# A fused attention, recurrence and expert kernel: 32 of 128 recurrence units moved into the attention rounds, expert rows scatter-added to the residual

## The reference, cut to what matters

```python
x = x + xattn0(layernorm(x), ctx, ...)      # q, k from ctx; softmax(q k'); mixes the columns of layernorm(x)
x = x + moe0(layernorm(x), ...)             # 16 experts, each token goes to its best 2
x = x + mamba(ctx, z=layernorm(x), ...)     # convolution, step sizes, recurrence over 512 positions, gate silu(z)
x = x + ffn1(layernorm(x), ...)             # two experts of 8, chosen once for all tokens, width 2048

def step(state, inp):                       # the recurrence, 16 states for each of 512 channels
    d, b, c, u = inp
    dA = jnp.exp(d[..., None] * A)
    state = state * dA + (d * u)[..., None] * b[:, None, :]
    y = jnp.einsum('bdn,bn->bd', state, c)
```

## Time and profile before

| | us |
|---|---|
| median of 3 runs | 1596.02 (1595.16 to 1596.70) |
| span of the profiled execution | 1594.7 |
| sequence stage (to the first routing step on DVE) | 262.2 |
| routing, to the first scan | 32.3 |
| the 8 units ahead | 28.1 |
| tile loop, 120 units | 429.7 |
| combine | 106.8 |
| from there to the end | 735.6 |

### The profile page before, as it was taken

One profiled execution on the slowest core, in us unless ns is written; L12 is line 12 of the kernel. 1 busy time (PEld: TensorE's weight loads), 2 busy tenths in 40 slices (PEclk: granted clock), 3 DMA queues, 4 the chain that ended last, 5 costly groups with the idle time before them and its releaser, 6 DMA issues.

```text
span 1594.7 us, 18873 instructions
## 1 busy us (share of the span) xinstructions
PE 1391.5 (87%) x6080; PEld 1030.4 (65%) x6080; DVE 936.9 (59%) x1186; ACT 709.8 (45%) x1303; POOL 784.0 (49%) x607
## 2 busy tenths in 40 slices
PE   6988983588899989897166999999999999999998
PEld 3535532566666656664166787878787887878786
DVE  2677767999999999998683224241414224241413
ACT  4445433266766776665143333333333333333332
POOL 0000000788888988885631445444544545444442
PEclk9898895699999999999555999999999999999999
DMA  3202214477977987863655900010000100010000
GB/s 105 108 26 81 107 53 165 158 240 257 315 257 234 319 269 264 281 198 125 218 198 203 364 14 0 0 66 1 14 0 13 52 13 0 0 53 0 0 0 26
DMA packets 78202, 191.29 MB, mean 120 GB/s; under 512 B 10856, under 2 KB 15752, under 8 KB 77120
## 3 DMA queue, kind: packets, MB, share of 16 engines
q1 hardware_dynamic: 64832, 157.03, 29.3%
q0 software_dynamic: 6400, 20.98, 4.1%
q10 hardware_dynamic: 6912, 12.59, 2.2%
HBM read 152.55 MB, written 38.01 MB: 119 GB/s over the span
## 4 chain that ended last, share of the span: by engine, by line
PE 58%; DVE 22%; issue 10%; ACT 4%; POOL 3%; DMA 3%; ACTq 0%; SPq 0%; DVEq 0%; POOLq 0%
PE decay L1675 22%; PE bank L1664 21%; DVE decay L1247 11%; DVE S L1256 4%; PE bank L1474 2%; PE decay L1430 2%; PE bank L1437 1%; DVE XH L1114 1%; PE bank L1494 1%; PE bank L1534 1%; PE decay L1484 1%; PE bank L1619 1%; POOL Y L767 1%; PE bank L1561 1%; PE decay L1480 1%
## 5 line engine op out<-in xcount | busy, mean ns | idle before, releaser
L1387 DVE CAST HFH<-HF 128x512 fp32r<-128x512 f32 x128 | 59.0, 461 | 496.7 <-ACT HF L1045 496.7
L815 POOL TENSOR_TENSOR W2L<-W2R,W2H 128x512 fp32r<-128x512 f32 x128 | 172.5, 1347 | 348.2 <-ACT W2H L1040 348.2
L728 POOL TENSOR_TENSOR S<-DTU,Bb 128x1024 f32<-128x1024 f32 x128 | 304.7, 2401 | 25.1 <-DVE row_hot L1229 21.7
L1247 DVE TENSOR_TENSOR_SCAN decay<-decay,S 128x1024 f32<-128x1024 f32 x128 | 292.9, 2288 | 0.5 <-ACT decay L892 0.5
L1664 PE MATMUL bank<-XSH,W1H 128*128 128x512 f32 x512 | 202.9, 396 | 4.2 <-POOL W1L L811 4.2
L1675 PE MATMUL decay<-W2H,HFH 128*128 128x512 f32 x512 | 200.4, 391 | 5.3 <-DVE HFL L1389 5.3
L1664 PE MATMUL bank<-XSH,W1L 128*128 128x512 f32 x512 | 203.0, 396 | 0.0
L1664 PE MATMUL bank<-XSL,W1H 128*128 128x512 f32 x512 | 202.3, 395 | 0.0
L1675 PE MATMUL decay<-W2L,HFH 128*128 128x512 f32 x512 | 199.9, 390 | 0.0
L1675 PE MATMUL decay<-W2H,HFL 128*128 128x512 f32 x512 | 199.7, 390 | 0.0
L811 POOL TENSOR_TENSOR W1L<-W1R,W1H 128x512 fp32r<-128x512 f32 x128 | 171.1, 1337 | 49.6 <-ACT W1H L1031 49.6
(11 more groups left out here) (212 smaller groups left out, 2102.3 us busy)
## 6 DMA issues: line engine op xcount, KB each, us to landing
WGU<-in_L_ffn_gate_w SPq DMA_DIRECT2D x48, 384.0 KB, 3.8
WGU<-in_L_ffn_up_w SPq DMA_DIRECT2D x48, 384.0 KB, 5.1
WD<-in_L_ffn_down_w SPq DMA_DIRECT2D x48, 384.0 KB, 4.9
Bb<-bc_rows SPq DMA_DIRECT2D x32, 512.0 KB, 7.9
Cb<-bc_rows SPq DMA_DIRECT2D x32, 512.0 KB, 9.7
...
```

The lines of the kernel that those rows point to most:

```text
L728: pool.tensor_tensor(S[u % NP][:], DTU[:, ds(b, 1), c, :].to_broadcast([P, PAIR, L]), Bb[j][:], ALU.mult).then_inc(dbu_ready, 1)
L815: pool.tensor_tensor(W2L[f % 2][:], W2R[:, ds(e, 1), f, :].rearrange("p e d -> p (e d)"), W2H[f % 2][:].bitcast(F32), ALU.subtract).then_i ...
L1247: dve.tensor_tensor_scan(flat, flat, S[u % NP][:].rearrange("p i l -> p (i l)"), 0.0, ALU.mult, ALU.add).then_inc(scan_done, 1)
```

## The change

The program is laid out anew as far as the combine stage.

- Batch 0's projections, convolution and step sizes run alone at the start. Then come 4 rounds, written out in place of the loop. Round b holds the attention of batch b, the recurrence inputs of batch b+1 (none in round 3), and 8 units of batch 0 (`ROUND`), 32 in all (`EARLY`).
- In the rounds PE uses three banks in turn for every product (`jobs`, `bank_of`); a job waits until the job three places ahead of it has been taken out. The four `decay` banks and YS are the units'.
- Both layer norms of a round are applied on ACT (4 instructions of 128x512 each) with a shift from POOL in place of DVE's. Of the step sizes' five passes DVE keeps two (`correction`); POOL has the other three (`step_sizes`), in its list ahead of the round's next unit but two.
- Units of batch 0 have four buffers of S, Bb and Cb, the later ones eight.
- Routing lays out the slot's token and its weight: 64 small DVE steps of 128x48 in place of four of 128x768, and a product of 96 columns in place of 48.
- 8 units still run ahead of the first tile, 80 are spread over the 48 tiles (1 or 2 each), 8 (`TAIL`) follow the last tile.
- x1 is stored as rows. A tile's result, scaled by the slot's weight, is added to those rows by an indirect accumulating DMA issued on POOL (`add_rows`), each of which waits for the one before. `store_y`, `gather_y`, `add_first`, `add_second` and the tile's copy of its index column are gone; four loads of 1 MB bring x2.

```diff
-PAD = 6200
+PAD = 14200
+TAIL = 8
+LATE = 5
...
+        EARLY = UB
+        ROUND = EARLY // B
+        AHEAD = EARLY + 2 * HP
         ALL = B * UB
-        cuts = [AHEAD + (ALL - AHEAD) * j // SLOT_TILES for j in range(SLOT_TILES + 1)]
+        cuts = [AHEAD + (ALL - AHEAD - TAIL) * j // SLOT_TILES for j in range(SLOT_TILES + 1)] + [ALL]
...
+        jobs = mamba_in(0) + mamba_out(0)
+        for b in range(B):
+            jobs += four("e", b)[:2] + four("v", b)[:2] + four("e", b)[2:] + four("v", b)[2:]
+            jobs += (mamba_in(b + 1) if b + 1 < B else []) + four("p", b) + four("o", b)
+            jobs += (mamba_out(b + 1) if b + 1 < B else []) + four("n", b) + [("score", b, 0)]
+        job_at = {job: i for i, job in enumerate(jobs)}
...
+            def step_sizes(b):
+
+                dt, dtu, rl = DT[:, b], DTU[:, b], XP[:, :, TAPS - 1:]
+                pool.wait_ge(nd_ready, b + 1)
+                pool.wait_ge(r_ready, b * DC + DC)
+                pool.tensor_tensor(rl, rl, ZZ[:], ALU.subtract).then_inc(size_made, 1)
+                pool.wait_ge(ln_ready, b + 1)
+                pool.wait_ge(size_made, 2 * b + 1)
+                pool.tensor_tensor(dt, rl, dt, ALU.add).then_inc(size_made, 1)
+                pool.wait_ge(size_made, 2 * b + 2)
+                pool.wait_ge(u_spilled, b * DMA + DMA)
+                pool.wait_ge(xd_ready, b + 1)
+                pool.tensor_tensor(dtu, dt, dtu, ALU.mult).then_inc(dt_ready, 1)
...
+            products(0, 3)
+            for b in range(B):
+                n = b * ROUND
+                products(n + 3, n + ROUND)
+                scale_and_shift1(2 * b + 2)
+                products(n + ROUND, n + ROUND + 2)
+                if b + 1 < B:
+                    scale_and_shift1(2 * b + 3)
+                    step_sizes(b + 1)
+                products(n + ROUND + 2, n + ROUND + 3)
...
+            def add_rows(j):
+
+                pool.wait_ge(yt_ready, j + 2)
+                if j:
+                    pool.wait_ge(yt_added, j * DMA)
+                pool.indirect_dma_start(out=x2_rows, out_offset=bass.IndirectOffsetOnAxis(ap=slot_dst[:, j:j + 1], axis=0),
+                                        in_=YT[j % 2][:], in_offset=None, compute_op=ALU.add).then_inc(yt_added, DMA)
...
                 gate_by_up(j)
+                if j >= 2:
+                    add_rows(j - 2)
                 if j + 2 < SLOT_TILES:
                     gather(0, j + 2)
-
-
-            def gather_y(b, k, count):
...
-                pool.tensor_copy(gcol[n % 2][:], slot_tok[:, ds(j, 1)]).then_inc(gcol_ready, 1)
-                wait_apart(pool, gcol_ready, j + 1)
...
-            def gather_y(b, k, count):
-
-                if b >= 2 and k == 0:
-                    pool.wait_ge(y_loaded[b % 2], b // 2 * (TOP * T * DMA))
-                pool.tensor_copy(pcol[b % 2][k][:], pos[:, k, b * T:(b + 1) * T]).then_inc(pcol_ready, 1)
-                pool.wait_ge(pcol_ready, count)
-                for t in range(T):
-                    pool.indirect_dma_start(
-                        out=(Y1, Y2)[k][b % 2][:, t, :], out_offset=None, in_=y_dram,
-                        in_offset=bass.IndirectOffsetOnAxis(ap=pcol[b % 2][k][:, t:t + 1], axis=0)).then_inc(y_loaded[b % 2], DMA)
...
+                decays(n + 5, n + 6)
+                if more:
+                    silu_u(b + 1)
+                decays(n + 6, n + 7)
+                if more:
+                    take_qk(b + 1)
+                    take_xd(b + 1)
+                decays(n + 7, n + 8)
+                norm_x1(b)
+                if more:
+                    size_abs(b + 1)
+                for t in range(T):
+                    take_turned("n", b, t, XNT)
+                if more:
+                    size_exp(b + 1)
+                take_scores(b)
+                if more:
+                    size_ln(b + 1)
+                    norm_x(b + 1)
+                decays(n + 8, n + 9)
...
-                act.activation(YT[:], DOWN[:], ACT.Copy, scale=0.5).then_inc(yt_ready, 1)
-
-            def store_y(j0, n):
-                j = j0 + n
-                act.wait_ge(yt_ready, j + 2)
-                act.dma_start(y_dram[ds(j * P, P), :], YT[:]).then_inc(yt_stored, DMA)
...
+                if j >= 2:
+                    act.wait_ge(yt_added, j * DMA - DMA)
+                act.activation(YT[n % 2][:], DOWN[:], ACT.Copy, scale=slot_w[:, j:j + 1]).then_inc(yt_ready, 1)
...
+                if more:
+                    convolve(b + 1, (2, 3))
+                unit(n + 5)
+                add_x(b, 0)
+                add_x(b, 1)
+                unit(n + 6)
+                add_x(b, 2)
+                add_x(b, 3)
+                statistics_x1(b)
+                unit(n + 7)
+                if more:
+                    positive_part(b + 1)
+                    statistics_x(b + 1)
+                    correction(b + 1)
...
+                for t in range(NT):
+                    dve.tensor_scalar(tile_hot[:, k, t, 0, :], iota_j[:], jf[:, k, t:t + 1], tokid[:, t:t + 1],
+                                      ALU.is_equal, ALU.mult)
+                    ins = dve.tensor_scalar(tile_hot[:, k, t, 1, :], iota_j[:], jf[:, k, t:t + 1], rwt[:, k, t:t + 1],
+                                            ALU.is_equal, ALU.mult)
+            ins.then_inc(hot_ready, 1)
...
-            def add_first(b):
-
-                dve.wait_ge(x1_loaded, max(b + 1, 2) * DMA)
-                dve.wait_ge(y_loaded[b % 2], (b // 2 + 1) * TOP * T * DMA)
-                x1 = X1[b % 2]
-                for t in range(T):
-                    dve.scalar_tensor_tensor(x1[:, t, :], Y1[b % 2][:, t, :], rwt[:, 0, b * T + t:b * T + t + 1], x1[:, t, :],
-                                             ALU.mult, ALU.add).then_inc(part_ready, 1)
...
+            def statistics_x2(b):
+
+                dve.wait_ge(x2_loaded[b], DMA)
+                statistics(X2[b], vare2[b % 2], means[b % 2], var2_ready)
```

994 lines of the change are left out of this document (566 added, 428 removed).

## The result

The changed kernel takes 1731.03 us (median of 4 runs, 1730.0 to 1736.2) against 1595.59 for the kernel before beside it: a ratio of 1.0856, 95% interval 1.0838 to 1.0873. It is slower by 8.6%. The profiled execution has a span of 1729.5 us, 134.8 more than before; the forecast was +73 (1669, range 1588 to 1750). The sign and the mechanism came out. The rise is 1.8 times the forecast: the sequence stage, routing and the tile loop came out 27, 13 and 20 us above it, the other stages within 2.

What follows compares the result with a forecast made beforehand. Before the change PE bounds the sequence stage and DVE the tile loop. Terms 102.6 + 6.5 + 1 - 28.9 + 31 - 39.0 = +73 on 1594.7 give 1669 us; own range 1640 to 1700, whole range 1588 to 1750.

Steps and rivals of the forecast that it cites:

- The start: Sequence stage before the first scan: nothing of batch 0 is hidden any more, so the first scan comes at 64.1 us.
- The rounds: Sequence stage: 82.4 us per full round from first scan to first scan, last one 53.5; stage +102.6.
- The chain: Path through the engines' lists in a round, followed through what waits last: 79.4 us before contention.
- the contention with POOL: DVE and POOL slow each other side by side: 3 us a round taken, between 0 and 11.
- Routing: Routing stage: four passes (9.95 us) go, 64 small steps add 6.4, contention with POOL 10: +6.5.
- The tile loop: Loop over 48 tiles with 80 units instead of 120: 8.35 us a tile, 401 in all, -28.9.
- the ring from the gate product over the gather to turn_x: Tile loop: dependency ring over two tiles, 15.6 to 17 us, no longer hidden by DVE's units; 8.35 us a tile taken.
- Tail, combine, ahead: 8 units behind the last tile +31; combine without additions and gathers -39.0; 8 units ahead of the first tile +1.
- (A): Rival, chance 0.16: tile loop at its fullest resource, 7.2 us a tile, no routing contention, rounds near 76; 1585.
- (B): Rival, chance 0.14: only the rounds' gain or only half of the tile loop's slack comes; 1628.
- (C): Rival, chance 0.12: DVE and POOL hold each other up at each meeting, +8 a round, +9 in routing; 1702.
- (D): Rival, chance 0.11: tile loop bound by adds, each waiting for the landing before it, 10 us a tile; 1748.

## Why the prediction was right, and where it was short

**The start (64.1, measured 70.0).** The convolution ended at 36.0 (35.6) and the step sizes took 10.6 (10.7). What was short is the product with xpT and the one with dtpT, which I had taken at 3.6 and some 3.7 us (4.8 with its copy) from rows of before; the stretch of the first has a granted clock of 1.00 there, the upper level. PE had nothing to do for 6.8 us while the convolution and Silu ran, and the stretch of the xpT product shows a granted clock of 0.59, between the levels of 1.2 and 2.4 GHz; the product took 6.1 us. PE's list there and that stretch:

```profile
38.86 6.10 PE L1649 MATMUL bank<-DTU,xpT 128*48 128x512 f32 x8 [6.81 <-ACT DTU L938]
45.63 5.60 PE L1655 MATMUL bank<-xdb,dtpT 16*128 16x512 f32 x8 [0.67 <-ACT xdb L944]
```

```profile
38.90:45.00 6.10, 6.07 (x8) 1.33 (x8) 0.00 (x0) 0.00 (x0) 0.00 (x0) 0.59 0.42 172
```

2.5 and 1.9 of the 5.9 us are these two. The durations of a row hold for the clock that it ran at, and PE's list, cut by more waits, ran at a lower mean clock: 0.79 in a round, where a batch had 0.88.

**The rounds (82.4, measured 88.1 on average).** The chain was right: 79.4 without contention, 77.8 measured with the products cut. The DVE idle places and their releasers were as described. The term that failed is the contention with POOL, taken as 3 us a round between 0 and 11: it is 10 to 12. My reason ("one such loss in ten of its instructions") had no row behind it; the upper end, a loss at each meeting, had four. Round 3's 57.4 against 53.5 is the same term, which I had left out there: 52.7 with the products cut.

**Routing (+6.5, measured +19.5).** The same term again, 10 taken between 0 and 19, 16.5 measured (30.3 less 64 x 0.215); and a small step costs 0.215 us and not 0.1, +7. I had argued that 64 steps lose little more than 4 did. It goes by the number of POOL instructions beside them, not by that of the steps.

**The tile loop (-28.9, measured -8.9).** The mechanism was right: DVE's idle time is no bound, the ring from the gate product over the gather to turn_x is; moving the gather alone gave 30 us. Its size was 8.77 and not 8.35 us a tile. One number that failed is the issue of the adding DMA, priced as a gather's (1.0 to 1.3): it is 1.60, with a gap of 0.3 behind it, ahead of the gather in the ring. That is 0.6 us in a ring over two tiles, so 0.3 of the missing 0.42; the rest was not followed.

**Tail, combine, ahead** (+31, -39, +1) measured +30.3, -37.2 and +0.9. In the combine a wait for a DMA replaced the one for gathers, as DVE's idle 4.26 and 3.58 us ahead of its third and fourth batch show.

**The rivals.** (A) is refuted: even with POOL's products cut the loop took 7.9 us a tile, at 0.94 of the DMA engines, and a round came near 77 only with the products of the rounds cut. (B) did not come. (C), contention at each meeting, came about nearly in full: of its +8 a round 7 to 9 came, of its +9 in routing 6.5. Its argument against, that scans and products run beside each other undisturbed, is true of scans and of products with C (2.29 and 1.22 us beside POOL, as before), whose decay operand lies in PSUM, and says nothing of the convolution and the small steps, whose operands all lie in SBUF. With (C) the forecast would have been 1702, and the loop's missing 20 us and the start's 6 make it 1728. (D) did not come: the adds land in 5.9 us, and POOL waited for them 21.6 us in all, in 9 of 47 cases. Yet it was for (D) alone that the stated range went up to 1750: the measured 1731 lies above 1700, the top of my own range, and above (C). That the range holds it is luck, since the 62 us above the forecast came from contention, small steps, the ring's size and the start, and none from what (D) stood for.

What stays open: how much of the loop each of its three limits costs where two act at once was not separated, which of the DMA engines, PE and the ring of adds sets the last one was not tested, and the 6 to 8 us by which the unchanged stages differ from execution to execution are not explained.
